# Third feed-forward of a four-layer network: second lane half a batch of phases behind the first, and two phases a tile for queries and keys

## What is computed

```
y = layernorm(x)
for l in range(2):                         # DEPTH
    h = shift_token(y)                     # second half of the columns comes from the row before
    q, k, v = split(h @ wqkv[l], 3)        # 8 heads of 64
    q, k = l2norm(q) * qs[l], l2norm(k) * ksc[l]
    q, k = rotary_xpos(q, k)
    # each block of 64 rows looks at itself and the block before, scale 8, causal band mask
    o = softmax(8 * q @ k.T + mask) @ v
    y = y + o @ wo[l]
    h = shift_token(y)
    h = (h - mean) / sqrt(var + 1e-5) * lg[l] + lb[l]
    a, g = split(h @ w1[l] + b1[l], 2)     # 341 columns each
    y = y + (a * gelu(g)) @ w2[l] + b2[l]
x = x + y
```

## Time and profile before

| | before |
|---|---|
| median of 3 runs | 5479.9 us |
| profiled execution | 5487.05 us, its span 5485.7 us |
| busy PE | 4046.9 us (74%) |
| busy DVE | 2918.3 us (53%) |
| busy ACT | 1911.6 us (35%) |
| busy POOL | 885.0 us (16%) |
| mean granted TensorE clock | 0.783 of full speed |

### The profile page before, as it was taken

The page is one execution under the profiler, slowest core; times in us unless marked ns, Lnnn a source line. Parts: engine busy times, 40 slices in busy tenths (PEclk is TensorE's granted clock), DMA queues, the critical chain, the costliest instruction groups (busy, mean ns, idle before and its releaser), DMA issues.

```text
span 5485.7 us, 96739 instructions
## 1 busy us (share of the span) xinstructions
PE 4046.9 (74%) x40667; PEld 3139.4 (57%) x40732; DVE 2918.3 (53%) x7893; ACT 1911.6 (35%) x4228; POOL 885.0 (16%) x664
## 2 busy tenths in 40 slices
PE   5786958367888888882757768586888888885398
PEld 4664848255556565552646556475555655565277
DVE  4545464425555545547255665646666666665232
ACT  3233232123333333330232332424555555552122
POOL 0000000231111101112600000002222211220534
PEclk7555565588999999985766666668999999997699
DMA  9200000150000000001210000000000000000255
GB/s 270 60 2 1 2 1 2 61 164 1 1 1 1 1 1 1 1 5 35 31 42 1 1 1 2 0 2 2 1 1 1 1 1 1 1 1 18 90 159 140
DMA packets 140868, 152.46 MB, mean 28 GB/s; under 512 B 7808, under 2 KB 128002, under 8 KB 139792
## 3 DMA queue, kind: packets, MB, share of 16 engines
q1 hardware_dynamic: 119024, 128.21, 7.9%
q0 software_dynamic: 21408, 18.05, 1.9%
HBM read 87.38 MB, written 59.76 MB: 27 GB/s over the span
## 4 chain that ended last, share of the span: by engine, by line
PE 29%; DVE 11%; ACT 7%; issue 2%; another core or an unknown queue 1%; POOL 0%; DMA 0%; SPq 0%; DVEq 0%; ACTq 0%; POOLq 0%
PE banks_lane L3108 3%; PE banks_lane L3719 3%; ACT work L3276 2%; PE banks_lane L3198 2%; PE banks_lane L810 2%; PE banks_lane L3155 2%; PE banks_lane L3185 2%; PE banks_lane L425 1%; DVE work L2822 1%; PE banks_lane L3172 1%; PE banks_lane L3212 1%; PE banks_lane L3712 1%; PE banks_lane L818 1%; PE banks_lane L2676 1%; PE banks_lane L2688 1%
## 5 line engine op out<-in xcount | busy, mean ns | idle before, releaser
L425 PE MATMUL banks_lane<-constants,work 128*128 128x128 f32 x968 | 186.3, 335 | 406.5 <-DVE work L411 161.2
L425 PEld LDWEIGHTS banks_lane<-constants,work 128*128 128x128 f32 x968 | 140.6, 173 | 476.4 <-DVE work L411 153.6
L405 POOL TENSOR_TENSOR weights<-weights,constants 128x4 f32<-128x4 f32 x76 | 78.5, 1033 | 1911.8 <-DVE weights L400 1911.8
L425 PE MATMUL banks_lane<-constants,weights 128*128 128x128 f32 x596 | 124.6, 345 | 349.8 <-DVE weights L411 94.3
L425 PEld LDWEIGHTS banks_lane<-constants,weights 128*128 128x128 f32 x596 | 88.2, 178 | 384.0 <-issue 160.6
L3276 ACT ACTIVATE work<-banks_lane,weights 128x192 f32<-128x192 f32 (+1 forms) x512 | 248.9, 505 | 134.7 <-DVE weights L3376 134.6
L405 POOL TENSOR_TENSOR work<-work,constants 128x4 f32<-128x4 f32 x76 | 77.3, 1018 | 1114.5 <-DVE work L400 1114.5
L3383 POOL TENSOR_TENSOR weights<-weights,constants 128x16 f32<-128x16 f32 x64 | 185.4, 2897 | 264.8 <-DVE weights L3288 264.8
L3198 PE MATMUL banks_lane<-constants,work 128*128 128x128 f32 x896 | 137.8, 300 | 88.6 <-ACT weights L3245 45.4
L2054 DVE TENSOR_REDUCE work<-banks_lane 128x2 f32<-128x512 f32 x256 | 158.8, 684 | 79.8 <-PE banks_lane L1915 79.6
L3372 DVE TENSOR_REDUCE weights<-banks_lane 128x2 f32<-128x384 f32 (+1 forms) x256 | 122.4, 520 | 139.9 <-PE banks_lane L3185 139.7
(11 more groups left out here) (790 smaller groups left out, 11144.4 us busy)
## 6 DMA issues: line engine op xcount, KB each, us to landing
work<-experts_dram_l_ffn SPq DMA_DIRECT2D x39, 964.0 KB
room_l_ffn<-work SPq DMA_DIRECT2D x30, 1188.0 KB, 14.1
work<-experts_dram_l_ffn SPq DMA_DIRECT2D x23, 512.0 KB
weights<-weights_dram SPq DMA_DIRECT2D x1, 4833.5 KB, 14.4
work<-room_l_ffn SPq DMA_DIRECT2D x36, 132.0 KB
weights<-weights_dram SPq DMA_DIRECT2D x1, 4112.0 KB, 12.8
weights<-bands_dram SPq DMA_DIRECT2D x1, 4096.0 KB, 13.7
weights<-room_l_ffn SPq DMA_DIRECT2D x26, 132.0 KB
```

Of the source, the lines that this page charges most:

```text
L405: pool.tensor_tensor(n.rstd, n.rstd, c("neghalf", cols=(0, n.rstd.shape[1])), ALU.pow).then_inc(*u.pool.step(name))
L425: done = pe.transpose(bank[0:rows, t * P:(t + 1) * P], block, c("ident"))
```

## The change

In the code of each engine a second yield, `keys{t}`, is added to a tile, so that a unit has 32 phases. For DVE the first phase ends after the query rotation and the second holds the key rotation and the query factor; for PE, ACT and POOL the second phase is empty, and their work of the tile stands where it stood. And the two lanes are woven with a lead of 15 phases: the first lane's first 15 phases stand alone, then phase 15 of the first lane is followed by phase 0 of the second, and so on; the second lane's last 15 phases stand alone at the end. No instruction of the computation is added or dropped. Loads of the activation tables are placed by the compiler, where the function wanted is in another set than the last.

```diff
+L2_FFN_LEAD = 15
@@ pe
                           ).then_inc(*u.pe.step(f"project{t}_{n}"))
             yield f"project{t}"
+            yield f"keys{t}"
             for n, bank in enumerate((b[3], b[2])):
@@ dve
                 if n == 0:
                     u.dve.mark(f"roped{t}_0")
+                    yield f"project{t}"
                     continue
                 dve.wait_ge(*u.dve.last())
                 dve.tensor_tensor(m.cos[:, 1, :], m.cos[:, 1, :], m.sin[:, 1, :], ALU.add).then_inc(*u.dve.step(f"roped{t}_1"))
             dve.wait_ge(*u.pool.at(f"roots{t}"))
             dve.tensor_scalar(m.q_factor[:, t, :], m.rn[:, t, 0, :], L2_FFN_QK_SCALE, None, ALU.mult).then_inc(*u.dve.step())
-            yield f"project{t}"
+            yield f"keys{t}"
@@ stage_l2_ffn
-    in_two_lanes(layers, run, units_of(run, [("l2_layer", n) for n in range(L2_FFN_DEPTH)]), lead=0)
+    in_two_lanes(layers, run, units_of(run, [("l2_layer", n) for n in range(L2_FFN_DEPTH)]), lead=L2_FFN_LEAD)
```

## The result

The changed kernel takes 5736.8 us (median of 3 runs, 5719.6 to 5743.4) against 5479.9: a ratio of 1.0464, interval 1.043 to 1.0498. The forecast was 5680 us, within 5530 to 5780.

What follows compares the result with a forecast made beforehand. Queue order, not PE at its limit, was taken to set the pace. The stage, 70 + 7 x 172 + 45 + 42 + 50 = 1411 us against 1211, adds 200 to 5487.05; the median lies 7 lower: 5680 us, range 5530 to 5780.

Steps and rivals of the forecast that it cites:

- The circles: Tiles beside the other lane's attention steps: project to next project 13.0 us in the first lane, 11.1 in the second.
- the clock: Allowance for PE matmuls slowed at the lower clock: between nothing and 44 us a period, taken as 7.
- The two tile stretches: One lane's four tiles beside the other's attention steps: 49.4 and 44.4 us, together 93.8 a period.
- The mixed stretches: One lane's scores and first attention steps beside the other's tail: 30.7 and 40.3 us at full clock.
- stretch 1: First lane's four tiles beside the second lane's attention steps: 49.4 us, PE's work filling some 65%.
- stretch 2: First lane's scores to step 2 beside the second's tail: 30.7 us, attention chain alone 23.9, PE some 64%.
- The ends: Lanes' unpaired phases and last stretches: 70 us at the start; 45, 42 and 50 after the seven periods.
- The table loads: ACT's table loads: 32, 16 more than before, 1.28 us each, 20.5 us more of ACT, counted inside the mixed stretches.
- stretch 4: Second lane's scores to step 3 beside the first's tail: 40.3 us, 30.4 alone, PE's work filling some 55%.
- An even filling: Rival: the stagger keeps PE supplied, a pair falls to 128 us, stage -108 us, 5372 us; chance 0.07.
- The longest chain: Rival: the tail fits into the attention chain's gaps, 23.9 and 30.4 us, kernel 5490 to 5560 us; chance 0.12.
- The clock stays low: Rival: idle stretches hold PE at the lower clock mostly, period about 195 us, kernel 5840 us; chance 0.11.

Runs made afterwards that it cites:

- the filling matmuls: 22 matmuls without a result a unit put in PE's waits: 5674.3 us in the changed kernel, 5468.2 us in the kernel before.
- both mendings: Changed kernel with the key copy moved from ACT to DVE and 22 matmuls without a result a unit: 5653.6 us, 1.0302.

## Why the forecast held, point by point

The stage became 252 us longer where 200 had been worked out. The circles and the order in the queues are as said; one term, the clock, was too small.

**The circles.** 13.0 and 11.1 us a tile were worked out. In tiles that ran at full clock 13.00, 12.82 and 11.03 were measured, and the key copy stands behind four exponentials as said. A unit's first tile took 14.61; its project ran at the lower clock, 5.49 instead of 2.84 us. Moving that copy and shifting by one phase moved the distances as the links say. The two tile stretches, 93.8 us by the sum, measured 96.2, and 94.9 with the filling matmuls.

**The mixed stretches.** 30.7 and 40.3 by the sum, 31.6 and 40.8 at full clock with the filling matmuls. The two long links in them, 10 and 12.4 by the sum, measured 9.75 and 13.1. In the kernel as it is, the third pair of up matmuls took 3.45 us at the lower clock where 1.75 had been put; with the filling matmuls it took 1.95.

**The clock is the term that was mis-sized.** 7 us a period were put for it. The four measured stretches lie 12.7 us above the links, and 10.3 of that are in the two mixed stretches, at 0.81 and 0.84. The prediction compared the stretches by PE's busy share, and that did not tell them apart: stretch 1, put at 65%, ran at 0.94, and stretch 2, put at 64%, at 0.81. Why these two differ no run shows. Over seven periods (1246.8 us, 178.1 each against 172) the excess is 43 of the 52 us that the stage is longer than forecast. The Trainium skill ("TensorE: Matmul & The Clock Gate", section "HAM oscillation — how this bites in real kernels") tells of short bursts between waits that each begin slow. The stretches at 0.81 and 0.84 and what the filling matmuls did to them agree with it, though the waits there are for DMA, and here for DVE and ACT, with the DMA share at 0.00.

**The ends.** First part 70.8 us against 70; the last part 145.8 against 45 + 42 + 50 = 137, the rest of the missing 52, at a clock of 0.85.

**The table loads.** 32, as said, of 1.283 us. One in four lies on the path in the period that I followed, the one ahead of the Gelus in stretch 4. The sum had also counted the one in stretch 2, and there the Gelu waits another 2.03 us for PE behind its load (4136.74 to 4140.05), so it cost nothing.

**Sums that do not hold.** The prediction called the new order 10 and 12 us worse a pair than today. For today it took the six later double steps at 8.6 us, 51.6, where the earlier trace rows has 61.9 for them; its parts of today add up to 143 us of a pair that takes 153.5. So the two comparisons are some 10 us too high together. The forecast was added up from the new stretches and does not use them. And "one more step, 30.4 alone" should be 30.7 (23.9 and 6.8).

**The rivals.** *An even filling* decides below a period of 143; it is 177.5 us from one shift copy of a lane to the next (4030.30 to 4207.81), and 173 to 181 over the periods in which both lanes run. PE is busy 75% of the stage, where about 70% was forecast, because its matmuls are slower and not because more are supplied. *The longest chain* wanted 23.9 us for stretch 2; it is 31.6 even at full clock. *The clock stays low*, with a period of 195, is the rival that came nearest: what the stage exceeds the forecast by is in the main its mechanism, at a quarter of the way from 172 to 195.

**The parts of the loss**, as far as the runs separate them: 187 of the 252 us lie in the seven periods and 65 in the ends. The filling matmuls took some 70 off the changed kernel's stage and 17 off the one before, so some 53 of the difference are the clock. The key copy behind the exponentials is worth 30, and both mendings together 84. The stage without 31 of the table loads was 22 shorter. What is left is the woven order at full clock, the mixed stretches above all, and the ends: it was worked out and read from the timeline, and no run took it apart further.

## What to carry to other kernels

Before two lanes are shifted against each other, follow each circle (what must end before the next tile or step may start) through every queue that it crosses, POOL's too, and write down whose work now stands ahead: here a lane's copy behind the other lane's exponentials made 13.0 us of a tile, and for tiles at full clock the links add up to the measured time to 0.2 us. The offset was to let one lane's waits be filled by the other's work; in these queues the waits on the circles became waits for both lanes. Where links have gaps, give the clock a wide range: stretches with the same forecast busy share ran at 0.94 and 0.81 here. And try matmuls without a result in the gaps first: they cost a few lines, took 69.7 us off the changed kernel's stage and 16.8 off the one before, and were worth more than any other mending here.

## What was not expected of the hardware

The filling matmuls: in stretch 2 PE was busy 26.65 of 35.21 us at a clock of 0.81, and with some 20 more matmuls 26.77 of 31.58 us at 1.00, so more matmuls took no more of PE's time. In the kernel before, the same matmuls raised the first steps from 0.67 and the tail from 0.87 to 1.00; the former became 2.4 us shorter, the latter did not. A raised clock gave time back only in some of the stretches where it rose.
